# Graph network layers on one core: two source tiles per step gathered by TensorE in float32r parts, W2 loaded late into row buffers

## The reference

```python
def layer(x, edge_attr, eps, We, be, W1, b1, gamma, beta, W2, b2):
    m = relu(x[src] + edge_attr @ We + be)            # 40000 x 512
    agg = segment_sum(m, dst, num_segments=1250)
    h = ((1.0 + eps) * x + agg) @ W1 + b1
    h = relu(batch_norm(h, gamma, beta))              # mean and variance over the nodes
    return relu(h @ W2 + b2)
```

## Time and profile before

| | us |
|---|---|
| median of 3 runs | 1784.39 |
| profiled execution | 1790.04 |
| its span | 1788.0 |
| PE busy | 1423.6 (80%) |
| DVE busy | 1223.6 (68%) |
| POOL busy | 1168.9 (65%) |
| ACT busy | 322.3 (18%) |

### The profile page before, as it was taken

How to read it: one execution, slowest core, us unless ns; L and a number is a source line. 1 busy time by engine, 2 the same in 40 slices (tenths; PEclk the granted TensorE clock), 3 DMA queues, 4 the chain that set the end, 5 groups by cost and what they waited for, 6 DMA issues and landing times.

```text
span 1788.0 us, 20050 instructions
## 1 busy us (share of the span) xinstructions
PE 1423.6 (80%) x6937; PEld 679.4 (38%) x7045; DVE 1223.6 (68%) x1899; ACT 322.3 (18%) x765; POOL 1168.9 (65%) x1235
## 2 busy tenths in 40 slices
PE   1798988989578888788947888777894888788888
PEld 1254444445223434333512434333451334333444
DVE  7877777775676676676566676677565666676657
ACT  3111111116301001011720010010181010010014
POOL 6777777770477777777057777777506777777740
PEclk9999999999789999998979899999996999998999
DMA  7877777772577777777167777777617777777753
GB/s 232 249 211 210 211 210 210 210 211 66 203 210 211 210 210 210 210 211 211 47 223 210 210 211 209 210 210 210 175 58 242 210 211 210 210 210 211 210 145 117
DMA packets 115319, 351.03 MB, mean 196 GB/s; under 512 B 22010, under 2 KB 23162, under 8 KB 115172
## 3 DMA queue, kind: packets, MB, share of 16 engines
q0 software_dynamic: 97280, 318.84, 61.9%
q1 hardware_dynamic: 17892, 30.36, 4.9%
HBM read 336.32 MB, written 12.80 MB: 195 GB/s over the span
## 4 chain that ended last, share of the span: by engine, by line
POOL 61%; issue 21%; PE 12%; DVE 3%; DMA 2%; POOLq 0%; ACT 0%; DVEq 0%; SPq 0%; ACTq 0%
POOL rows L443 61%; PE y_ps L1205 7%; PE pair_ps L1065 2%; PE h_ps L1154 1%; DMA rows<-node_table,src_all 1%; PE y_ps L1216 1%; DVE rows L738 1%; DMA node_table<-rows 1%; DVE rows L796 0%; DMA x_now<-x_pad 0%; PE y_ps L1165 0%; PE uT_ps L1143 0%; POOLq L353 0%; PE y_ps L1046 0%; PE uT_ps L1121 0%
## 5 line engine op out<-in xcount | busy, mean ns | idle before, releaser
L443 POOL DMA_INDIRECT rows<-node_table,src_all x1216 | 1153.6, 949 | 551.5 <-issue 550.9
L796 DVE SCALAR_TENSOR_TENSOR rows<-We_ps,negw_all,rows 128x512 f32<-128x512 f32 x1216 | 829.3, 745 | 452.5 <-DMA rows<-node_table,src_all 452.4
L1065 PE MATMUL pair_ps<-rows,onehot 128*64 128x512 f32 x2504 | 696.8, 679 | 300.3 <-DVE rows L796 298.9
L1065 PEld LDWEIGHTS pair_ps<-rows,onehot 128*64 128x64 f32 x2504 | 173.7, 148 | 651.6 <-issue 444.5
L1109 PE MATMUL y_ps<-table_parts,src_onehot 128*128 128x512 bf16 x980 | 246.9, 388 | 14.7 <-issue 13.2
L553 ACT COPY pair_sb<-pair_ps 128x512 f32<-128x512 f32 x80 | 46.5, 581 | 776.7 <-PE pair_ps L1065 776.6
L1109 PEld LDWEIGHTS y_ps<-table_parts,src_onehot 128*128 128x128 bf16 x1080 | 95.9, 100 | 227.7 <-issue 139.1
L1154 PEld LDWEIGHTS h_ps<-uT,W_sb 128*128 128x128 f32 x1184 | 137.8, 192 | 9.1 <-issue 4.5
L1154 PE MATMUL h_ps<-uT,W_sb 128*128 128x128 f32 x1184 | 139.4, 276 | 0.0
L1205 PE MATMUL y_ps<-W_sb,hT 128*128 128x512 f32 x288 | 124.7, 594 | 2.4 <-ACT hT L624 2.4
L559 ACT COPY uT<-uT_ps 128x512 f32<-128x512 f32 x40 | 23.5, 586 | 554.2 <-PE uT_ps L1143 554.2
(11 more groups left out here) (108 smaller groups left out, 699.0 us busy)
## 6 DMA issues: line engine op xcount, KB each, us to landing
rows<-node_table,src_all POOLq DMA_INDIRECT x1216, 3.7
W_sb<-W SPq DMA_DIRECT2D x8, 1024.0 KB, 8.4
node_table<-rows SPq DMA_DIRECT2D x29, 256.0 KB
x_now<-x_pad SPq DMA_DIRECT2D x5, 512.0 KB, 8.2
rows<-x_pad SPq DMA_DIRECT2D x5, 512.0 KB, 5.9
out<-rows SPq DMA_DIRECT2D x8, 256.0 KB
node_table<-rows SPq DMA_DIRECT2D x8, 224.0 KB
be_bc<-be SPq DMA_DIRECT2D x5, 256.0 KB, 13.7
```

Source lines behind the costliest of these rows:

```text
L443: nc.gpsimd.indirect_dma_start(rows[:, slot, :], None, table[:, :], bass.IndirectOffsetOnAxis(src_all[:, t:t + 1], 0)).then_inc(landed[q], 16)
L796: last = nc.vector.scalar_tensor_tensor(rows[:, slot, :], We_of, negw_all[:, t:t + 1], row, ALU.mult, ALU.max)
L1065: last = nc.tensor.matmul(pair_ps[h][WIN * win:WIN * (win + 1), :], onehot[:, h, tile - h * PAIR, :], rows[:, slot, :], start=t in firsts, ...
```

## The change

- Two tiles per step and in every step, the last of quad 3 and the last of quad 7, are gathered by PE: 20 a layer instead of 9. The gathers by DMA are 293 a layer instead of 304.
- The table is held as two float32r parts (ACT's copy and one subtraction) instead of three bf16 parts. A tile takes 20 products.
- They are made in the step itself: quads 0 to 2 for the tile of quad 3, quads 4 to 6 for that of quad 7; DVE makes a source one-hot behind quads 3 and 7.
- `product_h` moves from quad 5 to quad 3 and ACT's `finish_h` with it. In the last step `close_block` moves to quad 1, `finish_u` to quad 4, and the last block's `open_block` and `add_first_pair` to quad 5, and DVE takes the late statistics before the last quad.
- W2 has no buffer of its own: it is loaded into row slots 28 to 31 once step 8 is summed, and PE waits for it before the product with W2. The last step's quad 7 uses slot 26. `x` is reloaded into `x_now` at the end.
- At the start five spreads of source numbers instead of three, and twenty diagonals. `dst_all`, `w_all`, `rest` and `starts` lie in `hT`.

```diff
-    GATHERED = PAIR - 1
-    SHARE = [0, 0, 0, 0, 9, 3, 9, 9]
+    PARTS = 2
+    SHARE = [4, 8, 8, 0, 7, 7, 6, 0]
+    FINAL_SHARE = [4, 8, 8, 0, 10, 10, 0, 0]
...
+    W2_SLOT = STEP - 4
+    FINAL[7] = [(W2_SLOT - 2 + k, tile, win) for k, (_, tile, win) in enumerate(FINAL[7])]
...
-    def on_pe(i, tile):
-        return i > 0 and tile == GATHERED
+    ON_PE = [(quads[3][-1][1], quads[7][-1][1]) for quads in STEPS]
+    PE_TILES = 2 * BLOCKS
...
-        table_parts = sb("table_parts", [P, 3, BLOCKS, D], bf16)
-        src_bc = sb("src_bc", [P, BLOCKS - 1, P])
-        src_onehot = sb("src_onehot", [P, BLOCKS, P], bf16)
+        table_parts = sb("table_parts", [P, PARTS, BLOCKS, D], fp32r)
+        src_bc = sb("src_bc", [P, PE_TILES, P], mybir.dt.float16)
+        src_onehot = sb("src_onehot", [P, BLOCKS, P], fp32r)
-        W2_sb = sb("W2_sb", [P, C, D])
+        W2_sb = rows[:, W2_SLOT:W2_SLOT + C, :]
...
+        def hi_part(k):
+            b = ORDER[k]
+            nc.scalar.copy(table_parts[:, 0, b, :], table_stage(b)).then_inc(hi_ready, 1)
+        def lo_part(engine, ops, k, n, ready):
+            b = ORDER[k]
+            engine.wait_ge(hi_ready, n + k + 1)
+            ops.tensor_tensor(table_parts[:, 1, b, :], table_stage(b), table_parts[:, 0, b, :],
                               ALU.subtract).then_inc(ready, 1)
...
-                sp.dma_start(W2_sb[:, :, :], W2[...]).then_inc(params_loaded, 16)
+                wait_alone(sp, quad_summed[7], BLOCKS * (l + 1))
+                sp.dma_start(W2_sb, W2[...]).then_inc(W2_loaded, 16)
...
-                        if 1 < i:
-                            finish_h(n - 2, i - 2)
                         copy_pair(0, n, quad_summed[3], n + 2)
+                        if 0 < i:
+                            finish_h(n - 1, i - 1)
...
                     for q in range(4 * h, 4 * h + 4):
                         messages(q, l, i)
-                        if q == 3 and i < BLOCKS - 1:
-                            make_src_onehot(l, i + 1)
+                        k = 2 * i + h + 1
+                        if q in (3, 7) and k < PE_TILES:
+                            make_src_onehot(k)
...
-                        if q == 6:
+                        if q == (6 if i < BLOCKS - 1 else 4):
                             finish_u(n, u_ready)
+                        if q == 6 and i == BLOCKS - 1:
+                            dve.wait_ge(h_copied, n + 1)
+                            kept_stats(i)
+                            late_stats(BLOCKS, ...)
...
                     sum_quad(q, l, i)
-                    if i < BLOCKS - 1 and SHARE[q]:
-                        gather_share(q, l, i + 1)
...
-                        if q == 2:
+                        if q == (1 if final else 2):
                             close_block(n - 1)
-                        if q == 5:
+                        if q == 3:
                             product_h(n - 1, l)
+                    gather_share(q, l, i, FINAL_SHARE if final else SHARE)
+                    if q == 5 and final:
+                        open_block(n, l, i, True)
+                        add_first_pair(n)
...
-                if i == BLOCKS - 1:
-                    open_block(n, l, i, True)
-                    add_first_pair(n)
...
                 idle_products(uT_ps[:, :, :].rearrange("p c n -> p (c n)"), WARM)
+                pe.wait_ge(W2_loaded, 16 * (l + 1))
```

More of the change, by code:

```diff
@@ L28, in gnn_layers @@
     bf16 = mybir.dt.bfloat16
+    fp32r = mybir.dt.float32r
     i32 = mybir.dt.int32
@@ L75, in gnn_layers @@
     FINAL = quads_of(alternating, 0, [4] * 4) + quads_of(short, 1, [SHORT - 6, 3, 2, 1], SPLIT)
+    W2_SLOT = STEP - 4
+    FINAL[7] = [(W2_SLOT - 2 + k, tile, win) for k, (_, tile, win) in enumerate(FINAL[7])]
+    assert all(slot < W2_SLOT for quad in FINAL for slot, _, _ in quad)
+    assert len({slot for quad in FINAL for slot, _, _ in quad}) == LAST
     STEPS = [FULL] * (BLOCKS - 1) + [FINAL]
-    def on_pe(i, tile):
-        return i > 0 and tile == GATHERED
-    LANDINGS = [[16 * sum(not on_pe(i, tile) for _, tile, _ in quad) for quad in quads]
+    ON_PE = [(quads[3][-1][1], quads[7][-1][1]) for quads in STEPS]
+    PE_TILES = 2 * BLOCKS
+    LANDINGS = [[16 * sum(tile not in ON_PE[i] for _, tile, _ in quad) for quad in quads]
                 for i, quads in enumerate(STEPS)]
@@ L208, in gnn_layers @@
         tile_gathered = sem("tile_gathered")
-        early_split = [sem(f"early_split{k}") for k in range(2)]
-        split = [sem(f"split{k}") for k in range(4)]
+        hi_ready = sem("hi_ready")
+        lo_ready = sem("lo_ready")
+        early_lo_ready = sem("early_lo_ready")
+        W2_loaded = sem("W2_loaded")
         flag_ready = sem("flag_ready")
@@ L492, in _ @@
             nc.scalar.copy(We_ps[:, :], We_bc[:, :]).then_inc(We_ready, 1)
-            for k in range(EARLY, BLOCKS):
-                second_part(act, k, 0, split[1])
             act.wait_ge(w_parts_ready, 1)
@@ L512, in _ @@
             copy_w(1, last_pair_w)
-            for k in range(0, BLOCKS - 1, C):
-                some = min(C, BLOCKS - 1 - k)
+            for k in range(0, PE_TILES, C):
                 act.wait_ge(src_spread, k // C + 1)
-                nc.scalar.copy(src_bc[:, k:k + some, :].rearrange("q b p -> q (b p)"),
-                               y_ps[0][:, 0:some * P]).then_inc(src_bc_ready, 1)
+                nc.scalar.copy(src_bc[:, k:k + C, :].rearrange("q b p -> q (b p)"),
+                               y_ps[0][:, :]).then_inc(src_bc_ready, 1)
             for loaded in x_loaded:
@@ L1054, in _ @@
             pe.wait_ge(diag_ready, 1)
-            for k in range(3):
+            for k in range(PE_TILES // C):
                 spread_src(k)
@@ L1110, in gather_share @@
                                             start=(m == 0), stop=(m == len(products) - 1))
-                if start + SHARE[q] == len(products):
+                if share[q] and start + share[q] == len(products):
                     last.then_inc(tile_gathered, 1)
```

133 lines of the change are left out of this document (55 added, 78 removed).

## The result

The changed kernel takes 1902.9 us (median of 4 runs, 1900.3 to 1907.44) against 1784.22 for the kernel before (4 runs, 1783.86 to 1784.55): 1.0668 times as long, 95% interval 1.0647 to 1.0689. The prediction was 1790.4 us, 1745 to 1850. The side was right; the size, +118.7 us instead of +6, and the range were wrong. The profiled execution took 1900.3, its span is 1898.4, 110.4 more than before.

A forecast was written before the change was run, and what follows sets the result against it. It took POOL's issue of row gathers as the bound. Layers 1 to 3 gaining 28 us and layer 0 losing 34 made +6 on 1784.4, so 1790.4 us, range 1745 to 1850.

The forecast's parts named there:

- The unit of POOL's gain: Gather issue on POOL: eleven gathers fewer a layer at 1.253 us, 13.8 us a layer wherever POOL stays the bound.
- The start: Start of layer 0: gathers start about 3 us earlier, last src copy ends about 54.2, PE's first sum about 61.3.
- The end of a later layer: Layers 1 to 3: close 17.2 to 17.8 us behind the last gather instead of 13.2, net -9.5 a layer.
- The round trip itself: One step from PE to DVE and back: 36.6 us at full clock, 39.8 in layer 0, against POOL's 37.6.
- in layers 1 to 3 it just fits: Layers 1 to 3: a step's PE and DVE round of 36.6 us stays under POOL's 37.6, so POOL keeps the pace.
- I take 0.222: PE's float32r gather product over 512 columns: 0.222 us, with 0.433 and 0.866 kept for the range.
- The clock, counted as 0: PE in layers 1 to 3: the 36.6 us round was worked at full clock, with nothing added for a lower one.
- second rival: The round trip decides in all layers, through a product of 0.26 or half clock after pauses: about 1820 to 1830, 17%.
- The clock as a percentage: PE in layer 0: 0 to 3% of 385 us plus some 2.5 for slow first sums, taken as +7 us.
- at nothing: W2's late load into row slots and x reloaded into x_now: no cost, though W2 may delay rows 0 to 2 us a layer.
- Its own signs: Profile signs of being wrong: float32r products over 0.25, no POOL wait in layer 0, steps over 38 us in layer 2.

The follow-up runs named there:

- e3_third: The changed kernel with each tile's 20 products in quads 0 and 1 or 4 and 5, ten each: 1777.4 us, 0.9967 of the kernel before.
- e1_again: The changed kernel with the two table parts and the source one-hots in bf16 instead of float32r: 1828.8 us, 1.0256 of the kernel before.

## Why the prediction was right and wrong

**Held.** The unit of POOL's gain, where POOL leads: 44 gathers fewer, at 1.25 each (e3_third). The start: gathers from 22.88 (forecast about 23), first pair sum at 60.61 (61.3), last copy of src ended at 53.35 (54.2). The end of a later layer, within 1 us, in e3_third: -8.7 to -10.7 for -9.5, and 17.7 to 18.6 behind the last gather for 17.2 to 17.8. The round trip itself, named as what matters: 37.0 by its working, 36.86 measured in e1_again where the sums ran at full speed. That a float32r product costs about one bf16 product and not a multiple of it: 0.24, not 0.433 or 0.866. The Trainium skill (FP8 and Floating Point Precision, TensorE Precision Notes), which had given the lower price, agrees; its rule on the fast weight load (TensorE: Matmul & The Clock Gate, Weight-path perf modes) shows in the loads, 193 ns for float32r and 101 for bf16, but not in the time of a product.

**Failed: "in layers 1 to 3 it just fits".** The forecast put 36.6 beside POOL's 37.6 and gave the case that it doesn't fit 17%. Both allowances that it leaned on were too small. The product, "I take 0.222": the float32r burst measured 0.24 a product and 0.15 a burst, +1.6 a step, more than the 1.0 us of room by itself. Part of the burst's extra stood in the trace of before: nine bf16 products ahead of a sum (one record is missing) took 2.05 us, from 308.79 to 310.84, where 0.222 each makes 2.00. The three of the earlier trace rows, from which 0.222 was read, stood ahead of the W1 product.

```profile
308.79 2.12 PE L1109 MATMUL y_ps<-table_parts,src_onehot 128*128 128x512 bf16 x8
310.84 1.94 PE L1065 MATMUL pair_ps<-rows,onehot 128*64 128x512 f32 x8
```

The clock, counted as 0 in these layers: 2.8 a step. 36.6 + 1.6 + 2.8 = 41.0, measured 40.9 where the sum is fully slow and 39.3 to 39.7 where it is partly so. That is the forecast's own second rival with a price of 4.4 us a step instead of 1.9, and in place of -9.5 a layer it gave +17.5: 27 a layer, 81 us.

**Failed: the clock as a percentage, and the same product price, in layer 0.** The close came at 479.0 instead of 446.8 + 7, and the layer cost +58.9 instead of +34: another 25 us. Steps 1 to 8 lasted 40.0 to 44.8, mean 42.6 instead of 39.5. Some 16 of the 25 are again the product, 1.6 in each of ten steps; the other 9 are the clock. For it the forecast took 0 to 3% from the mean granted clock of whole stretches, 7 us with the first sums. With the pause filled layer 0 closes at 463.2, so the clock cost about 16. It isn't spread over the step: it falls behind the pause of 3.32 us, which is on the round trip, in five of the eight steps, and in four of them PE is slow again behind the placing of the weights. The prediction had the row of such a pause before it (seven sums at 3.65 behind 6.17) and charged it once, 2.5 us at the start, where its own round trip had a pause in each step.

81 + 25 is 106, and the end of the kernel, 0.9 shorter than before, takes one off. The other 8 of the 113 missed lie in the comparison: the profiled execution of before lay 5.7 over its median, that of the change 2.6 under.

**Failed, small: W2 and storage "at nothing".** Alone they cost 4.2 us (1.6 to 5 by the interval), within the bound of 2 a layer that was kept.

**Its own signs.** Of the signs of being wrong that the prediction named, one came: steps over 38 us in layer 2 (39.3 to 40.9). POOL did wait for pair sums in layer 0, but the close at 479.0 lay outside its 440 to 455.

**The range.** It reached to a product of 0.27 at full clock. The two terms were bounded one by one, but not together: at 0.24 and a slow sum the same working gives a round of 41.0, which is what was measured.

**Open.** Why the sum behind the same pause is slow, fully or partly, in step after step of the change's layers 1 to 3, but only in some steps of its layer 0 and in every second of e1_again; where the 4 us of the storage part lie. The full clock and bf16 together in the change's order were not run.

## What to carry to other kernels

When a product moves from the step ahead into the step that consumes it, add up the round trip of both engines and compare its margin with the sum of all small prices on it, not with each; 1 us of room in 37 was none here. Charge a lowered clock where the pause is, as a term of the loop, and try to put the producer a stage earlier before making it cheaper: here the order was worth 127 us, and once it was right the cheaper product and the full clock were worth 11 and 4. Work that computes nothing can pay for itself if it closes a pause on the critical loop: 83 us there, 4 once the loop no longer led.

## What the runs showed of the hardware

- float32r products of 512 columns follow each other 0.24 us apart, bf16 ones 0.2175; a burst among f32 sums costs 0.15 and 0.09 on top (change and e1_again). With 256 columns it is 0.12 and 0.11. The recorded weight loads of 193 and 101 ns set no floor.
- In the change's layers 1 to 3 a pause of PE of 3.32 us is followed by a sum at the lower clock, up to 3.61 us for 1.87, with a granted clock of 0.50; in the step shown full speed was back by 663.2. In layer 0 the same pause is followed by a full-speed sum in three of steps 1 to 8. Twelve products in the pause avoid it in all steps but the first of each layer; the mean granted clock of the kernel went from 0.929 to 0.977.
- In layer 0 of the change, in four of steps 1 to 8, eight products of 512 columns behind 18 products of one column each took 3.36 to 3.57 us instead of 2.05, with no pause of PE before them; in the step shown the granted clock was 0.54 (190.36 to 193.81).
